# Seven half-size products for eight in a dense layer of 2048 tokens, on one core

## The chip, the cores and the metric

One core of a Trainium2 chip runs the whole kernel in one launch. The metric is the device time of one execution in microseconds (us), lower is better. All arithmetic keeps float32 accuracy: each matrix product is done as three products of halves of the operands (see below).

## The reference, cut to what matters

Two blocks, each added to its input. The first is a layernorm, a convolution of width 3 from 1024 to 768 channels, attention in blocks of 128 tokens with 16 heads of 64, and two projections. The second, which the change is about, is a layernorm and a dense layer with a gated low-rank term:

```python
y = jnp.einsum('bth,oh->bto', x, W_base) + b_base          # x: 2048 tokens x 1024, W_base 1024 x 1024
A = lora_A[active]; Bm = lora_B[active]                    # 4 active experts of 16, rank 8
z = jnp.einsum('bth,erh->bter', x, A)
contribs = jnp.einsum('bter,eor->bteo', z, Bm) * 2.0
logits = (jnp.einsum('bth,eh->bte', x, router_W) + router_b)[..., active]
alpha = jax.nn.softmax(jnp.log(domain_prior[active] + 1e-12) + logits, axis=-1)
return y + jnp.einsum('bteo,bte->bto', contribs, alpha)
# and outside: x1 = x + attention(layernorm(x));  out = x1 + this(layernorm(x1))
```

## The kernel before

Five instruction streams are written out by hand, one for each engine and one (SP) that issues DMAs; semaphores join them, and nothing reorders them. In order of time they do:

1. Layernorm, transposition and convolution (to some 260 us).
2. The attention, with eight groups of 256 tokens, each with eight pairs of heads. The function `attention_pair(D)` exists on TensorE (PE), VectorE (DVE), ScalarE (ACT) and GpSimd (POOL); each calls it for D = 1, 2, ..., and a call takes some 9.5 us. On DVE it does, in this order, `masked` (L1024), `heads_low` (`oT_lo`, L1036), `unit_out` (L1063, L1069), `reciprocals` (L1032), and at D = 5 and 6 `pw_lo` (L1114). PE waits for `oT_lo` before `output_sums` (L1457 to L1459). SP runs `attention_step(g, i)` (L432), two steps to one D, which issues loads and stores at fixed steps: `c_raw` of the next group at i = 7, the weights `W_base` (8 DMAs, L448) at (4, 0), and the gate's weights (L450 to L459) at (5, 0). The last are four groups of four DMAs, and each group reads the expert's number from `act_sb` into a register first.
3. The dense layer, in 16 tiles of 128 tokens. The normalised tile is turned on DVE (L1172) from `x1g` into `fxT`, and then split in two halves for PE: `xT_hi` by ACT (L775) and `xT_lo` by DVE (L1147). The weights are split in the same way into `fw_hi` (ACT) and `fw_lo` (DVE, L1206). They have 1060 columns: 36 for the gate (32 of the low-rank A, 4 of the router) and 1024 of `W_base`. `dense(t, b)` multiplies tile t by block b of the columns (354, 354 and 352 wide) with `three_pass`:

```python
pe.matmul(out, a_hi, b_hi, ...)   # L63
pe.matmul(out, a_lo, b_hi, ...)   # L64 (the order of the factors depends on the caller)
pe.matmul(out, a_hi, b_lo, ...)   # L65
```

That is 8 chunks x 3 blocks x 3 = 72 matmuls a tile. The gate's columns are in block 0. When it is done, DVE and ACT compute the softmax and the scaled z (L1180 to L1195) into `azs`; PE turns it (L1571), ACT copies it to `azsT`, and three matmuls with `b_stack` (L1578) add the low-rank term and the bias. DVE adds x1 (`tile_outputs`, L1202) into `y`, and POOL stores it (L586). `group_moments` (L1558) is a small matmul that spreads a tile's mean and scale over the layout of `x1g`; its input goes DVE `tile_statistics`, POOL `tile_power` (L533), DVE. `tile_transposes` turns tiles 0 and 1 on PE. SP loads a tile twice, as rows (`load_tile`, L419) and in groups (`load_groups`, L429).

Of the kernel before, what the change touches and what calls it, by code (L numbers as in the profile page):

```python
# [6 lines left out]
F32 = mybir.dt.float32  # L7
# [6 lines left out]
P = 128  # L14
# [10 lines left out]
EPS = 1e-5  # L25
# [62 lines left out]
def network(nc, ident, x, conv_w, conv_b, wq, wk, wv, wo, pw, bq, bk, bv, bo, pb, w_base, b_base, lora_a, lora_b, router_w, router_b,  # L88
            prior, active, c_dram, m_dram, x1, out):
# [66 lines left out]
    WZ = Z + DM  # L156
    NB = 3
    COLS = ((0, 354), (354, 708), (708, WZ))
    OFF = (Z, 0, 0)
    OUT = tuple((lo + off - Z, hi - Z) for (lo, hi), off in zip(COLS, OFF))  # L160
# [5 lines left out]

    def row(c):

        return (c - SOON) % DC

    with ExitStack() as ctx:
# [61 lines left out]
                                                               ("fxn_0", [P, DM], F32)))  # L233
        c_hi = (c0_hi, c1_hi)
# [3 lines left out]
        x1t_2, x1t_3 = place(nc, SH, (("x1t_2", [P, DM], F32), ("x1t_3", [P, DM], F32)))  # L238
        fw_hi, = place(nc, CY + 2 * size_of([P, MC, GT]) - size_of([P, DC, WZ]), (("fw_hi", [P, DC, WZ], F32R),))
        x1t = (x1t_0, x1t_1, x1t_2, x1t_3)  # L240
        fxn_1, rep, gmask, spread, gs = place(nc, XL, (("fxn_1", [P, DM], F32), ("rep", [P, P], F32), ("gmask", [P, TG], F32),
                                                       ("spread", [P, 2, TG, 2], F32), ("gs", [P, 2, TG, 2], F32)))
        x1g_0, x1g_1 = place(nc, XH + 4 * CHUNK, (("x1g_0", [P, TG, DM // TG], F32), ("x1g_1", [P, TG, DM // TG], F32)))
        x1g = (x1g_0, x1g_1)
        fxT, = place(nc, XH + 5 * CHUNK, (("fxT", [P, DM], F32),))
        fxn = (fxn_0, fxn_1)
        xT_hi, xT_lo = place(nc, XH + 2 * CHUNK, (("xT_hi", [P, 2, DC, P], F32R), ("xT_lo", [P, 2, DC, P], F32R)))
        y, = place(nc, XL + 2 * CHUNK, (("y", [P, 2, DM], F32),))
        b_raw, b_hi, b_lo, b_stack = place(nc, XH, (("b_raw", [ER + 1, DM], F32), ("b_hi", [ER + 1, DM], F32R), ("b_lo", [ER + 1, DM], F32R),
                                                    ("b_stack", [KB, DM], F32R)))  # L250

# [11 lines left out]
        tp = ((psum[:, 0], psum[:, 6]),) + ((psum[:, 0], psum[:, 3]),)  # L263
        yp = (tuple(psum[:, b] for b in (1, 2, 4)), tuple(psum[:, b] for b in (5, 6, 3)))
# [16 lines left out]
                 "active_loaded", "az_loaded", "b_loaded", "fw_loaded", "az_split_hi", "az_split_lo", "b_split_hi", "b_split_lo",  # L281
                 "b_stacked", "fw_hi_ready", "fw_lo_ready", "logp_in", "logp_ready", "lsum_ready",
                 "fstats_done", "fmv_done", "fvar_ready", "frstd_ready", "fxn_ready", "fturned", "xT_hi_ready", "xT_lo_ready",
                 "spread_ready", "gp_done", "gs_ready", "z_done", "logit_ready", "fmax_ready", "fexp_ready", "rec_ready", "alpha_ready", "az_ready", "azs_hi_ready", "azs_ready",
                 "azT_done", "azsT_ready", "y_done", "y_ready")
        s = {n: sp.sem(n) for n in names}
        f_loaded = [sp.sem(f"f_loaded{i}") for i in range(XS)]
# [45 lines left out]
        def by_group(a, t):  # L333
            return a.rearrange("p c t -> p (c t)") if t < BLOCKED else a.rearrange("p c (g q) -> p c g q", g=TG)
# [1299 lines left out]
```

## Time and profile before

| | us |
|---|---|
| median of 3 runs (lowest, highest) | 786.25 (786.21, 786.28) |
| the profiled execution, its own time | 786.38 |
| its span in the trace | 784.5 |
| PE busy in the span | 765.6 (98%) |
| DVE busy | 524.7 (67%) |
| ACT busy | 382.3 (49%) |
| POOL busy | 165.5 (21%) |
| dense layer, from its first products to the end | about 575 to 784.5 |

The span is measured in the trace from the first to the last recorded work; the execution's own time lies 1.9 us around it. "Busy" counts overlapping matmuls as one stretch. A row of the timeline gives the start and the length of one or more instructions of a kind; matmuls overlap, so their cost is the distance from one start to the next, not the length.

### The profile page before, as it was taken

To read this page: it belongs to the slowest core of one execution; us is meant where nothing else is said; L and a number is where in the kernel's file an instruction comes from. 1 tells how busy PE (TensorE), PEld (TensorE's weight loads), DVE (VectorE), ACT (ScalarE), POOL (GpSimd) and SP (SyncE) were. 2 spreads that over 40 slices of the span, in tenths; PEclk is the share of its full clock that TensorE was granted. 3 is DMA by queue.
4 is the path that set the end of the run, shared out by engine and by line. 5 is a ranking of instruction groups with operands and counts; after the bars stand their busy time and mean duration, and the time that the engine had idled before them with its cause. 6 is when DMAs were issued, how large, how long until landed. Compare 5 with 4: busy or idle time off the path is not lost.

```text
span 784.5 us, 14391 instructions
## 1 busy us (share of the span) xinstructions
PE 765.6 (98%) x5182; PEld 693.8 (88%) x5182; DVE 524.7 (67%) x1506; ACT 382.3 (49%) x1046; POOL 165.5 (21%) x170
## 2 busy tenths in 40 slices
PE   4999999999999999999999999999999999999996
PEld 3898888888888889989999989899889999999996
DVE  6999996889887966454544445545787666767652
ACT  5953442344344887676767676767950111111010
POOL 2300100000000236252535344352401111111100
PEclk9999999999999999999999999999999999999999
DMA  8846834434446230403072332102254443525301
GB/s 329 287 123 176 271 116 133 170 127 161 156 153 242 88 122 1 148 2 140 10 265 99 99 112 96 55 33 78 95 152 146 147 136 107 158 85 162 108 28 54
DMA packets 49435, 101.39 MB, mean 129 GB/s; under 512 B 10195, under 2 KB 26451, under 8 KB 48084
## 3 DMA queue, kind: packets, MB, share of 16 engines
q1 hardware_dynamic: 47060, 92.08, 35.5%
q0 software_dynamic: 2304, 8.39, 2.6%
q8 instruction: 42, 0.69, 0.4%
q14 instruction: 29, 0.24, 0.1%
HBM read 73.97 MB, written 26.08 MB: 128 GB/s over the span
## 4 chain that ended last, share of the span: by engine, by line
PE 93%; DVE 3%; ACT 2%; issue 1%; DMA 0%; POOL 0%; DVEq 0%; POOLq 0%
PE net_psum L63 21%; PE net_psum L65 21%; PE net_psum L64 21%; PE net_psum L1342 11%; PE net_psum L1404 4%; PE net_psum L1415 4%; PE net_psum L1427 4%; PE net_psum L1457 2%; PE net_psum L1458 2%; PE net_psum L1459 2%; PE net_psum L1326 1%; PE net_psum L1578 1%; ACT pr L683 1%; ACT xn L609 1%; DMA xn<-in_x 0%
## 5 line engine op out<-in xcount | busy, mean ns | idle before, releaser
L63 PE MATMUL net_psum<-fw_hi,xT_hi 128*128 128x354 f32 (+1 forms) x384 | 127.2, 331 | 0.4 <-DVE fw_lo L1206 0.4
L64 PE MATMUL net_psum<-fw_lo,xT_hi 128*128 128x354 f32 (+1 forms) x384 | 124.2, 324 | 0.0
L65 PE MATMUL net_psum<-fw_hi,xT_lo 128*128 128x354 f32 (+1 forms) x384 | 124.2, 323 | 0.0
L547 POOL TENSOR_TENSOR pr<-pr,rrec 128x512 f32<-128x512 f32 x64 | 66.6, 1042 | 209.2 <-DVE rrec L1032 206.1
L683 ACT ACTIVATE pr<-pr,negmax 128x128 f32<-128x128 f32 x256 | 99.0, 395 | 1.0 <-DVE negmax L1024 1.0
L1342 PE MATMUL net_psum<-ua,wa 128*128 128x256 f32 x384 | 83.8, 379 | 0.5 <-DVE ua L914 0.5
L1024 DVE CUSTOM_DVE_ANT_0 pr<-net_psum,mask 128x128 f32<-128x128 f32 x256 | 57.2, 288 | 37.9 <-PE net_psum L1404 37.8
L1342 PEld LDWEIGHTS net_psum<-ua,wa 128*128 128x128 f32 x384 | 72.6, 190 | 10.3 <-issue 0.7
L63 PE MATMUL net_psum<-x_hi,w_hi 128*128 128x512 f32 x192 | 76.4, 398 | 0.0
L64 PE MATMUL net_psum<-x_lo,w_hi 128*128 128x512 f32 x192 | 76.2, 397 | 0.0
L65 PE MATMUL net_psum<-x_hi,w_lo 128*128 128x512 f32 x192 | 75.6, 394 | 0.0
L63 PE MATMUL net_psum<-c_hi,wqk_hi 128*128 128x256 f32 x256 | 74.2, 290 | 0.0
L63 PEld LDWEIGHTS net_psum<-fw_hi,xT_hi 128*128 128x128 f32 x384 | 72.2, 188 | 1.5 <-DVE fw_lo L1206 0.8
L64 PEld LDWEIGHTS net_psum<-fw_lo,xT_hi 128*128 128x128 f32 x384 | 72.4, 189 | 0.0
L65 PEld LDWEIGHTS net_psum<-fw_hi,xT_lo 128*128 128x128 f32 x384 | 72.3, 188 | 0.0
L64 PE MATMUL net_psum<-c_lo,wqk_hi 128*128 128x256 f32 x256 | 71.6, 280 | 0.0
L65 PE MATMUL net_psum<-c_hi,wqk_lo 128*128 128x256 f32 x256 | 71.6, 280 | 0.0
L775 ACT ACTIVATE xT_hi<-fxT 128x512 fp32r<-128x512 f32 x28 | 16.1, 625 | 110.8 <-DVE fxT L1172 110.8
L640 ACT ACTIVATE w_hi<-raw 128x1024 fp32r<-128x1024 f32 x24 | 25.5, 1062 | 85.1 <-PE net_psum L65 76.7
L702 ACT ACTIVATE oT_hi<-net_psum,net_bv_c 128x256 fp32r<-128x256 f32 x64 | 26.9, 472 | 56.9 <-PE net_psum L1415 56.9
L1202 DVE TENSOR_TENSOR y<-net_psum,x1t 128x318 f32<-128x318 f32 (+2 forms) x48 | 21.7, 508 | 47.8 <-PE net_psum L1578 47.8
L683 ACT ACTIVATION_READ_ACCUMULATOR pr<-pr,negmax 128x1 f32 x256 | 49.7, 194 | 0.0
(194 smaller groups left out, 1772.3 us busy)
## 6 DMA issues: line engine op xcount, KB each, us to landing
wa<-in_conv_w SPq DMA_DIRECT2D x24, 512.0 KB, 4.1
raw<-in_conv_w SPq DMA_DIRECT2D x24, 384.0 KB, 4.2
xn<-in_x SPq DMA_DIRECT2D x16, 512.0 KB, 10.2
xr<-in_x SPq DMA_DIRECT2D x8, 1024.0 KB, 5.0
x_scratch<-xr SPq DMA_DIRECT2D x8, 1024.0 KB, 4.1
x1t<-x_scratch SPq DMA_DIRECT2D x16, 512.0 KB, 4.1
out<-y POOLq DMA_DIRECT2D x16, 512.0 KB, 5.0
x1g<-x_scratch SPq DMA_DIRECT2D x56, 128.0 KB, 3.2
```

The source lines that it names most:

```text
L63: pe.matmul(out, w_hi, x_hi, start=first, stop=False)
L64: pe.matmul(out, w_hi, x_lo, start=False, stop=False)
L65: return pe.matmul(out, w_lo, x_hi, start=False, stop=last)
L547: pool.tensor_tensor(pr[:, jj % 4], pr[:, jj % 4], rrec[:, jj % 4].unsqueeze(2).to_broadcast([P, UN, P]), ALU.mult).then_inc(s["p_ready"], 1)
L640: act.activation(w_hi[:, k % WR], raw[:, k % RR, 1:5], ACT.Copy).then_inc(s["w_hi_ready"], 1)
L683: e = act.activation(pr[:, jj % 4, un], pr[:, jj % 4, un], ACT.Exp, bias=negmax[:, jj % 2, un:un + 1], scale=-1.0, accum_out=rsum[:, jj % ...
L702: act.activation(oT_hi[:, jj % 2], op[:, jj % 2].rearrange("p b t -> p (b t)"), ACT.Identity, bias=bv_c[:, jj % NP:jj % NP + 1]).then_inc( ...
L1024: m = dve.tensor_tensor_reduce(out=pr[:, jj % 4, un], in0=scp[:, h, jj % 2 * GT + b * P:jj % 2 * GT + (b + 1) * P], in1=mask[:], scale=-DH ...
L1342: mm = pe.matmul(duo_acc(d, mi)[:, v * QUADS:(v + 1) * QUADS], wa[:, a % AW, mi, 1 - v, c % 2], ua[:, c, v, n * QUADS:(n + 1) * QUADS], st ...
L1404: mm = pe.matmul(scp[:, h, o], qf[e, jj % 2, t], kf[e, jj % 2, t], start=True, stop=True)
L1415: mm = pe.matmul(op[h * DH:(h + 1) * DH, jj % 2, b], vf[:, b, j * P + h * DH:j * P + (h + 1) * DH], pT[:, jj % 2, b, h * P:(h + 1) * P], s ...
L1427: mm = pe.transpose(ptp[jj % 2][:, un * P:(un + 1) * P], pr[:, jj % 4, un], ident[:])
```

## The change

The first CL = 4 tiles run as before, with blocks of 284, 512 and 264 columns. The other 12 run as NQ = 6 pairs. A pair's product is seen as a 2 x 2 matrix of blocks (two tiles by two halves of the 1024 channels) times a 2 x 2 matrix (two halves of the channels by two halves of the columns, 532 each: 18 + 512 and two of padding), and done with seven products of blocks instead of eight (the Strassen-Winograd scheme). The products are named A11, S1, S2, A12, S3, A22, S4 by their left operand; the S ones are sums and differences of turned tiles, made on DVE (`operand_sum`), and their right factors for S1, S2, S3, and for S4, are differences of blocks of the weights. The results are added in pieces by `pair_sum` on DVE, in place in the x1 tile, and stored from there.

The sums of the weights are made during the attention, one chunk each in `attention_pair(6)` to `(21)` (`weight_sum` and `low_sum` on DVE, `high_sum` on ACT), stored to DRAM by SP, and loaded again after the attention. For that the weights `W_base` and the gate's weights are loaded at SP's step (1, 0), and `gate_weights` on DVE copies the gate's columns into place in `attention_pair(5)`. The statistics of paired tiles move from DVE to ACT (`tile_moments`) and POOL (`pair_moments`), the scaling from DVE to ACT (`pair_scale`).

The diff, cut to its core:

```diff
@@ SP: attention_step
-                if (g, i) == (4, 0):
-                    for c in range(DC):
-                        sync.dma_start(fw_raw[:, row(c), Z:WZ], w_base[:, c]).then_inc(s["fw_loaded"], 16)
-                if (g, i) == (5, 0):
-                    sync.dma_start(act_sb[:], active).then_inc(s["active_loaded"], 16)
+                k = (NP * g + i) // 2 - TFIRST - 1
+                if i % 2 and 0 <= k < TSUMS:
+                    store_sum(k)
+                if (g, i) == (5, 7):
+                    for k in range(2):
+                        sync.wait_ge(t_stored[k], 16 * TSUMS)
                     load_tile(0)
                     load_tile(1)
+                if (g, i) == (1, 0):
+                    sync.dma_start(act_sb[:], active).then_inc(s["active_loaded"], 16)
+                    for c in range(DC):
+                        for (lo, hi), off, (left, right) in zip(COLS, OFF, OUT):
+                            sync.dma_start(fw_raw[:, row(c), lo + off:lo + off + right - left], w_base[:, c, left:right]).then_inc(s["fw_loaded"], 16)
                     sync.wait_ge(s["active_loaded"], 16)
                     for e in range(E_ACT):
@@ SP: after the attention
-            for t in range(XS, TT):
+            load_sums(0)
...
+            load_sums(1)
+            load_sums(2)
+            load_pair(0)
+            load_pair(1)
+            load_sums(3)
+            for q in range(2, NQ):
+                load_pair(q)
+            for n, (t, j) in enumerate(((TT - 2, 0), (TT - 2, 1), (TT - 1, 0), (TT - 1, 1))):
+                lo, hi = ((0, 2 * YW), (2 * YW, DM))[j]
+                sync.wait_ge(s["y_ready"], summed(NQ - 1, n + 5))
+                sync.dma_start(out[t * P:(t + 1) * P, lo:hi], x1t[x_slot(t)][:, lo:hi]).then_inc(s["last_stored"], 16)
@@ POOL
-            for t in range(TT):
-                if t + 2 < TT:
+            for t in range(CL):
+                if t + 2 < CL:
                     tile_power(t + 2)
                 store(t)
+                if t == CL - 2:
+                    pair_moments(0)
@@ DVE: attention_pair
+                if D == TFIRST - 1:
+                    gate_weights()
+                if 0 <= D - TFIRST < TSUMS:
+                    weight_sum(D - TFIRST)
+                if 0 <= D - TFIRST - 1 < TSUMS:
+                    low_sum(D - TFIRST - 1)
                 if D in (5, 6):
                     dve.wait_ge(s["pw_hi_ready"], D - 4)
+            def gate_weights():
+                dve.wait_ge(s["az_loaded"], 64 * E_ACT)
+                dve.memset(fw_raw[:, :, 3 * QW - PAD:3 * QW + PAD], 0.0)
+                half, pair = ER // 2, E_ACT // 2
+                for h in range(2):
+                    dve.tensor_copy(fw_raw[:, :, QW * h:QW * h + half], a_raw[:, :, half * h:half * h + half])
+                    z = dve.tensor_copy(fw_raw[:, :, QW * h + half:QW * h + ZW], r_raw[:, pair * h:pair * h + pair].rearrange("p e c -> p c e"))
@@ DVE: the pairs
+            for q in range(NQ):
+                more = q + 1 < NQ
+                a = CL + 2 * q
+                if q:
+                    pair_sum(q - 1, 5)
+                    pair_sum(q - 1, 6)
+                low_operand(q, S2)
+                pair_sum(q, 1)
+                low_operand(q, A12)
+                operand_sum(q, S4)
+                pair_sum(q, 2)
+                low_operand(q, S3)
+                if q:
+                    pair_sum(q - 1, 7)
+                    pair_sum(q - 1, 8)
+                low_operand(q, A22)
+                pair_sum(q, 3)
+                low_operand(q, S4)
+                if more:
+                    pair_turn(q + 1, 0)
+                pair_sum(q, 4)
+                if more:
+                    pair_turn(q + 1, 1)
+                    operand_sum(q + 1, S1)
+                gate_scores(a)
+                if more:
+                    low_operand(q + 1, A11)
+                    operand_sum(q + 1, S3)
+                gate_inputs(a)
...
@@ PE
+            def product(q, o, bank, chunks=range(DC // 2)):
...
+                for c in chunks:
+                    for h in range(2):
...
+                        pe.matmul(to, x_hi, b_hi, start=c == 0 and o in (A11, S1, A12), stop=False, skip_group_check=True)
+                        pe.matmul(to, x_hi, b_lo, start=False, stop=False, skip_group_check=True)
+                        mm = pe.matmul(to, x_lo, b_hi, start=False, stop=c == DC // 2 - 1, skip_group_check=True)
...
+            for q in range(NQ):
+                a = CL + 2 * q
+                product(q, A11, XB)
+                if q:
+                    gate_turn(a - 1)
...
+                product(q, S1, ZB)
+                if q:
+                    low_rank(q - 1, 1)
+                product(q, S2, XB)
+                if q + 1 < NQ:
+                    pair_moments(q + 1)
+                product(q, A12, YB, range(0, 2))
+                product(q, S3, XB)
+                product(q, A12, YB, range(2, 4))
+                product(q, A22, XB)
+                product(q, S4, ZB, range(0, 2))
+                gate_turn(a)
+                product(q, S4, ZB, range(2, 4))
+                low_rank(q, 0)
+            gate_turn(TT - 1)
+            low_rank(NQ - 1, 1)
```

On SP's queue, behind the load of group 2's `c_raw`, before:

```order
L370 DMA c_raw<-c_scratch 128x6x256 [waits net_c_lo_ready,net_c_stored]
L438 DMA pb_r<-in_pb 128x1024
L440 DMA xr<-in_x 128x2x1024
L370 DMA c_raw<-c_scratch 128x6x256 [waits net_c_lo_ready]
L435 DMA x_scratch<-xr 128x2x1024 [waits net_x1_ready]
```

and after (eight triples of `fw_raw` stand there, and four groups from L608 to L612, of which the last has no other behind it but L585):

```order
L472 DMA c_raw<-c_scratch 128x6x256 [waits net_c_lo_ready,net_c_stored]
L602 DMA act_sb<-in_active 1x4
L605 DMA fw_raw<-in_w_base 128x248
L605 DMA fw_raw<-in_w_base 128x512
L605 DMA fw_raw<-in_w_base 128x264
...
L608 TENSOR_LOAD act_sb [waits net_active_loaded]
L609 DMA a_raw<-in_lora_a 128x8x8
L610 DMA r_raw<-in_router_w 128x8
L611 DMA lbias<-in_router_b 128x1
L612 DMA lbias<-in_prior 128x1
...
```

The loads for the gate have moved from behind the fifth group to here, ahead of `pb_r` and the first `xr`.

On DVE, in `attention_pair(5)`, before:

```order
L1032 RECIPROCAL rrec<-rsum 128x4 [waits net_p_ready,net_exp_ready] x2
L1063 COPY vf<-net_psum 128x512 [waits net_v_done]
L1114 TENSOR_TENSOR pw_lo<-pw_raw,pw_hi 128x1024 [waits net_pw_hi_ready]
L1024 ISA pr,negmax<-net_psum,mask 128x128 [waits net_pT_done,net_sc_done]
L1024 ISA negmax 128x1
```

and after:

```order
L1310 RECIPROCAL rrec<-rsum 128x4 [waits net_p_ready,net_exp_ready] x2
L1341 COPY vf<-net_psum 128x512 [waits net_v_done]
L1403 MEMSET fw_raw 128x8x4 [waits net_az_loaded]
L1406 COPY fw_raw<-a_raw 128x8x16
L1407 COPY fw_raw<-r_raw 128x8x2
L1406 COPY fw_raw<-a_raw 128x8x16
L1407 COPY fw_raw<-r_raw 128x8x2
L1398 TENSOR_TENSOR pw_lo<-pw_raw,pw_hi 128x1024 [waits net_pw_hi_ready]
L1302 ISA pr,negmax<-net_psum,mask 128x128 [waits net_pT_done,net_sc_done]
```

Five instructions and a wait for all sixteen gate loads now stand ahead of `pw_lo` and of the next masks.

On PE, the end of the program before (the last of the matmuls with 352 columns, and the low-rank term):

```order
L63 MATMUL net_psum<-fw_hi,xT_hi 128x352
L64 MATMUL net_psum<-fw_lo,xT_hi 128x352
L65 MATMUL net_psum<-fw_hi,xT_lo 128x352
L1578 MATMUL net_psum<-b_stack,azsT 128x318 [waits net_azsT_ready]
L1578 MATMUL net_psum<-b_stack,azsT 128x354
L1578 MATMUL net_psum<-b_stack,azsT 128x352
```

and after (266 columns a matmul; L2016 is the transposition of the last tile's `azs`):

```order
L2003 MATMUL net_psum<-fw_hi,xT_lo 128x266
L2027 MATMUL net_psum<-b_stack,azsT 128x248 [waits net_azsT_ready]
L2027 MATMUL net_psum<-b_stack,azsT 128x248
L2027 MATMUL net_psum<-b_stack,azsT 128x264 x2
L2016 MATMUL net_psum<-ident,azs 98x128 [waits net_y_ready,net_azs_ready]
L2027 MATMUL net_psum<-b_stack,azsT 128x248 [waits net_azsT_ready]
L2027 MATMUL net_psum<-b_stack,azsT 128x248
L2027 MATMUL net_psum<-b_stack,azsT 128x264 x2
```

The last tile's transposition stands behind the last product, with nothing left to run beside it.

## Rows read from the trace of the kernel before

**Rows 1.** The chain that ended last, share of the span by engine (the page).

```profile
PE 93%; DVE 3%; ACT 2%; issue 1%; DMA 0%; POOL 0%; DVEq 0%; POOLq 0%
```

**Rows 2.** Window of one tile: length; busy (count) by engine; PEclk, DMA, GB/s.

```profile
653.90:666.34 12.44, 12.44 (x80) 12.40 (x79) 8.19 (x25) 1.71 (x5) 1.60 (x2) 1.00 0.45 126
```

**Rows 3.** Timeline of PE, tile 6: start, length, line, op, names, shapes, count.

```profile
654.54 0.32 PE L65 MATMUL net_psum<-fw_hi,xT_lo 128*128 128x354 f32 x1
...
661.85 0.33 PE L65 MATMUL net_psum<-fw_hi,xT_lo 128*128 128x354 f32 x1
```

**Rows 4.** Timeline of PE, matmuls of 256 columns in the attention.

```profile
347.53 0.28 PE L64 MATMUL net_psum<-c_lo,wqk_hi 128*128 128x256 f32 x1
...
348.71 0.28 PE L65 MATMUL net_psum<-c_hi,wqk_lo 128*128 128x256 f32 x1
```

**Rows 5.** Groups of DVE, 614 to 733 us: count | busy, mean ns | idle before.

```profile
L1172 DVE STREAM_TRANSPOSE fxT<-x1g 128x1024 f32<-128x1024 f32 x10 | 12.4, 1245 | 0.9
L1147 DVE TENSOR_TENSOR xT_lo<-fxT,xT_hi 128x512 fp32r<-128x512 f32 x18 | 11.5, 683 | 0.0
```

**Rows 6.** Timeline of DVE, the gate of tile 8, from its scores to `azs`.

```profile
683.21 0.16 DVE L1180 TENSOR_TENSOR logit<-net_psum,lsum 128x4 f32<-128x4 f32 x1 [0.25 <-PE net_psum L65]
...
684.45 0.16 DVE L1184 RECIPROCAL erec<-esum 128x1 f32<-128x1 f32 x1 [0.89 <-ACT expl L779]
...
685.36 0.19 DVE L1195 TENSOR_TENSOR azs<-az,azs 128x32 fp32r<-128x32 f32 x1
```

**Rows 7.** Timeline of PE, the end of dense(0, 0).

```profile
575.03 0.43 PE L63 MATMUL net_psum<-fw_hi,xT_hi 128*128 128x354 f32 x1 [0.38 <-DVE fw_lo L1206]
```

**Rows 8.** Timeline of POOL: one tile's moments, and the store of tile 2.

```profile
27.83 0.19 POOL L511 TENSOR_SCALAR cvareps<-csq 128x1 f32<-128x1 f32 x1 [0.44 <-ACT junk L602]
...
29.05 0.19 POOL L515 TENSOR_TENSOR cshift<-csum,crstd 128x1 f32<-128x1 f32 x1
...
618.18 0.67 POOL L586 DMA_DIRECT2D out<-y  x1 [4.67 <-DVE y L1202]
```

**Rows 9.** DMA issues of the page: kind, count, KB, us from issue to landing.

```profile
x1t<-x_scratch SPq DMA_DIRECT2D x16, 512.0 KB, 4.1
```

**Rows 10.** Group of ACT, 0 to 60 us.

```profile
L602 ACT ACTIVATE junk<-xn,csum 128x1024 f32<-128x1024 f32 x4 | 4.6, 1151 | 0.1
```

**Rows 11.** Timeline of POOL, the last store.

```profile
779.80 0.53 POOL L586 DMA_DIRECT2D out<-y  x1 [11.69 <-DVE y L1202]
```

**Rows 12.** Timeline of SP: start, length of the issues, line, names, count.

```profile
275.23 0.37 SPq L370 DMA_DIRECT2D c_raw<-c_scratch  x1
...
397.26 4.23 SPq L448 DMA_DIRECT2D fw_raw<-in_w_base  x8
...
443.17 0.69 SPq L456 DMA_DIRECT2D a_raw<-in_lora_a  x1
...
455.05 0.38 SPq L459 DMA_DIRECT2D lbias<-in_prior  x1
```

**Rows 13.** DMA issues, as in rows 9, of the last of the gate's loads.

```profile
lbias<-in_prior SPq DMA_DIRECT2D x4, 0.5 KB, 2.5
```

**Rows 14.** Timeline of DVE in `attention_pair(5)` and `(6)`.

```profile
293.07 1.71 DVE L1114 TENSOR_TENSOR pw_lo<-pw_raw,pw_hi 128x1024 fp32r<-128x1024 f32 x1
...
296.54 0.88 DVE L1036 SCALAR_TENSOR_TENSOR oT_lo<-net_psum,net_bv_c,oT_hi 128x256 fp32r<-128x256 f32 x2
```

**Rows 15.** Timeline of PE, the first matmul that reads that `oT_lo`'s tile.

```profile
302.10 0.28 PE L1457 MATMUL net_psum<-oT_hi,wo_hi 128*128 128x256 f32 x1
```

**Rows 16.** Windows of 1 us behind the last matmul, columns as in rows 2.

```profile
781.00:782.00 1.00, 0.00 (x0) 0.00 (x0) 0.00 (x0) 0.00 (x0) 0.00 (x0) 0.99 0.98 406
782.00:783.00 1.00, 0.00 (x0) 0.00 (x0) 0.00 (x0) 0.00 (x0) 0.00 (x0) 0.50 0.17 70
```

**Rows 17.** Timeline of SP at the start of the kernel.

```profile
9.13 7.21 SPq L345 DMA_DIRECT2D xn<-in_x  x8
```

More of the change, by code:

```diff
@@ L250, in network @@
                                                     ("b_stack", [KB, DM], F32R)))
+        t_rows = []
+        for name, at, count in (("t_v", XL + 3 * CHUNK, 13), ("t_p", XL, 5), ("t_b", XH, 5), ("t_f", XL + 6 * CHUNK + 3 * size_of([P, DM]), 1)):
+            t_rows += place(nc, at, [(f"{name}{i}", [P, 2 * QW], F32R) for i in range(count)])
         psum = sp.ps("psum", [P, 8, BANK])
@@ L850, in _ @@
+            for t in range(CL):
+                if t and t + 1 < CL:
                     tile_xT(t + 1)
@@ L1558, in group_moments, with pair_moments @@
                 pe.matmul(gp, rep[:], spread[:, t % 2], start=True, stop=True).then_inc(s["gp_done"], 1)
-            for t in range(TT):
+            def pair_moments(q):
+                pe.wait_ge(s["spread_ready"], CL - BLOCKED + 2 * (q + 1))
+                pe.wait_ge(s["gs_ready"], CL - BLOCKED + q)
+                if q:
+                    pe.wait_ge(s["y_ready"], summed(q - 2, 7) if q > 1 else NB * CL)
+                pe.matmul(gpq[q % 2], rep[:], spread[:].rearrange("p k g v -> p (k g v)"), start=True, stop=True).then_inc(s["gp_done"], 1)
@@ new lines, in low_rank @@
+            def low_rank(q, k):
+                t = CL + 2 * q + k
+                pe.wait_ge(s["azsT_ready"], t + 1)
+                for j in range(2):
+                    new = k == 1 and j == 1
+                    bank = xyz[1 - q % 2][XB] if new and q == NQ - 1 else xyz[q % 2][((YB, ZB), (XB, YB))[k][j]]
+                    for h in range(2):
+                        cols = slice(YW * h, YW * h + YW) if j == 0 else slice(2 * YW + RW * h, 2 * YW + RW * h + RW)
+                        mm = pe.matmul(bank_half(bank, j)[:, h], azsT[:, t % 2], b_stack[:, cols], start=new, stop=True, skip_group_check=True)
+                    mm.then_inc(s["y_done"], 1)
@@ L1561, in _ @@
+            for t in range(CL):
                 if t:
-                    if t + 1 < TT:
+                    if t + 1 < CL:
                         group_moments(t + 1)
                     dense(t, 0)
+                    if t == CL - 1:
+                        pair_moments(0)
                     dense(t, 1)
```

464 lines of the change are left out of this document (397 added, 67 removed).

## The prediction, made before the changed kernel had run

> **What bounds the kernel now.** I read the chain of waits first: 93% of the span goes through PE [rows 1]. Then the window of one dense tile: PE is busy for all of its 12.44 us, DVE for 8.2, ACT for 1.7 and POOL for 1.6 [rows 2]. So the dense layer is worth what its matmuls take, and there is room on the other engines. Next the distances between matmuls. With 354 columns 45 intervals take 661.85 - 654.54 = 7.31 us, 0.162 us each [rows 3]; with 256 columns 10 intervals take 1.18 us, 0.118 each [rows 4]. Every one of these has its own weight load, so the price goes by columns: 0.00045 us a column, and 0.1225 us for 266 columns.
>
> **Six pairs of tiles.** Before, a pair costs 2 x 12.44 = 24.89 us. Of one tile's 12.44, the 72 products take 11.7, three low-rank matmuls 3 x 0.16 = 0.5, and what is left for a transposition and a moments matmul is 0.27. Now a pair has 7 x 4 x 2 x 3 = 168 products of 266 columns instead of 144 of 353: 168 x 0.1225 = 20.58. With 8 low-rank matmuls of some 256 columns (8 x 0.119 = 0.95), two transpositions and one moments matmul (0.4 by the 0.27 above), the PE work is 21.9 us.
>
> Does DVE keep up? It gets 7 `low_operand`, 4 `operand_sum` and 8 `pair_sum` of about 512 columns, 19 x 0.64 = 12.2 us at 11.5/18 each [rows 5], two turns of 1.25 [rows 5], and the small gate operations, 1.7 for each tile (0.5 for the scores, 1.1 from the reciprocal to `azs`, plus 0.1 for an operation more [rows 6]): 18 of 22 us. That fits on average, so only the order can hurt. I laid the four streams out with these durations. The tightest place is the gate's transposition in the middle of product S4. PE comes to it 19.9 us into the pair (156 products, four low-rank matmuls, the moments and one transposition: 156 x 0.1225 + 0.5 + 0.2 + 0.1). The input that starts DVE's last stretch is product S3, which ends at 14.0; behind it stand `pair_sum(4)`, a turn, a sum, the scores, `low_operand`, a sum and the gate's inputs: 4 x 0.64 + 1.25 + 0.5 + 1.2 = 5.5 us. Started at 14.2, it would be 0.2 us early; but DVE comes to it 0.4 us late by the operations ahead, so PE waits 0.2 to 0.3 us a pair. I take 22.2 us a pair: 6 x (24.89 - 22.2) = **-16.1 us**. ACT has 14 of 22 us, and its sums hide behind PE. Bounds: with no wait -18; with DVE's operations a tenth longer the hand order gives 0.35 us of wait a pair, with a fifth 0.85, and a stop of 1.5 a pair gives -8.
>
> By the Trainium skill ("TensorE: Matmul & The Clock Gate", the list of what overlaps and what doesn't in the part on packing) a weight load overlaps matmuls "only when row_grp differs". All the loads here use every row, so by that rule each of the 24 additional loads of a pair would stand in PE's way. The rows speak against it: 256-column matmuls, each with a load of its own, start every 118 ns [rows 4], which leaves no time for an unhidden load. By the rule the result would be rival E below.
>
> **The way into the pairs: +4.0 us.** dense(0, 0) already waits 0.38 us for the last `fw_lo` [rows 7]. It is now 284 columns wide, some 0.75 us shorter, but ends by the same `fw_lo`: +0.7. In tile 3 PE comes to `pair_moments(0)` at about 620.0. On POOL its two tiles stand behind the store of tile 2, issued 618.18 to 618.85 [rows 8], and take 1.4 us each for three operations (27.83 to 29.24 [rows 8]) and 0.3 for the `spread`: 618.9 + 3.4 = 622.3, which PE waits for, +2.1. The second, `pair_moments(1)`, needs tile 7, whose load is issued when tile 3's outputs are done (about 633.1 by then), lands 4.1 us later [rows 9], goes through two passes of 1.15 us on ACT [rows 10] and 1.8 on POOL: 641.3, against 640.1 for PE, +1.2. The sums of the weights for S4 land about 640.8 and are wanted at 646: nothing. New widths in the single tiles move the number of columns by none and the number of matmuls by none: nothing, +-0.5. Bounds of the whole: +0.7 to +6.
>
> **The end: +0.7 us.** The last transposition, the copy to `azsT` and the low-rank matmuls of the last tile have no product beside them (0.75 us); against this the tile is stored in halves by SP rather than whole by POOL, whose issue took 0.53 [rows 11]. Bounds 0 to +1.5.
>
> **The attention: +6.7 us.** SP issues the load of `c_raw` at 275.23 and is free at 275.6 [rows 12]. Now `act_sb` and 24 DMAs of `W_base` come next. They take 0.37 (the `c_raw` row) to 0.53 us (4.23/8 for the same tensor [rows 12]); I take 0.45 between them: 276.1 + 24 x 0.45 = 286.9. Then come the four groups with register reads. From the first `a_raw` to the end of the last issue they took 455.43 - 443.17 = 12.3 us [rows 12], to which come about 0.9 us of reads ahead of the first and 2.5 us to the last landing [rows 13], in all 15.3 to 15.7. So all sixteen have landed at 302.2 to 302.9. DVE comes to `gate_weights`, which waits for them, at 293.07, where `pw_lo` stood before [rows 14]. It waits 9 to 10 us. Behind that instruction stand the gate's copies (0.75 us, an estimate from their 256 and 32 columns at the rate of rows 5), then the row of before again: `pw_lo` and eight masks, 296.54 - 293.07 = 3.5, less 0.2 as the masks no longer wait, and `oT_lo`, 0.87 [rows 14]. PE wants this for `output_sums` at 302.10 [rows 15] and gets it at 302.3 + 0.75 + 3.3 + 0.87 = 307.2: **+5.1**. With 0.37 and 0.53 an issue it is 2.7 and 7. The first `weight_sum` (532 columns) and the second `pw_lo` then stand ahead of `a_lo`, which a projection needs: +0.8 (0 to 1.5). From D = 6 to 22 DVE has 1.2 us more a call, which fits into idle stretches, and ACT 0.55: nothing.
>
> In such a stop PE's clock may fall. At the end of the run the granted clock is 0.99 in the window that ends 782 and 0.50 in the next [rows 16], the lower of its two levels (1.2 of 2.4 GHz), after PE had done nothing since its last matmul at 778.4. A stop of 5 us may end with the clock low; then the matmuls behind it take up to twice their time until it rises again. What that costs is not in these rows: estimate +0.8, bounds 0 and 3.
>
> **Sum.** -16.1 + 4.0 + 0.7 + 5.1 + 0.8 + 0.8 = -4.7. From the profiled execution's 786.38 that gives 781.7, and the median lies 0.13 under it: **781.5 us**.
>
> **The rivals.**
>
> B. The gate's loads are not waited for to any effect: SP issues faster, or PE's own reserve takes it up. For it speaks the 9 us between DVE's `pw_lo` and PE's `output_sums` [rows 14, 15]; against it that the wait is as long. Then the attention costs nothing: 786.25 - 16.1 + 4.0 + 0.7 = 774.8 us.
>
> C. The other side: SP issues at the rate at which it issued `xn`, 7.21/8 = 0.9 us a DMA [rows 17], since all 24 loads of `W_base` are queued at once, 4.3 MB. Each 0.1 us an issue moves the landing and so PE by 2.4 us. At 0.9 PE is 10.8 us later than in the forecast: 792.3. From 0.65 us an issue on the change is slower than the kernel before. Against it: eight of these loads, four times the size of the small ones, took 0.53 each [rows 12].
>
> D. The pairs are limited by DVE, not PE. If the operations on the stretch before the transposition take more than in rows 5 (two sources of PSUM, strided pieces), each pair stops for 1.5 us more: 781.5 + 9 = 790.5. For it: the chain has 0.2 us to spare only. Against it: rows 5 hold operations with strided sources already.
>
> E. The weight loads count: a matmul cannot start sooner than 0.14 us after the last one, between the 0.118 of rows 4 and the 0.162 of rows 3, however few its columns. Then a pair costs 168 x 0.14 + 1.35 = 24.9 us, as before, and the result is 781.5 + 16 = 797.5. Against it: the interval of rows 4 itself.
>
> By the skill's page of above a load of 128 columns takes 107 ns (P / 1.2 GHz); 24 more of them a pair would be 2.6 us, and the result 797, an estimate from that page's figure.
>
> **How the numbers follow.** Forecast (A) 0.52, with its own range 777 to 786; B 0.27; C 0.10; D 0.08; E 0.03. A measurement of this kernel tells 0.2% (1.6 us) from no change. By its bounds A is faster in 0.46, no change in 0.05 and slower in 0.01; B is faster; C and D have 0.02 and 0.01 of no change, where their price is half as large, and are slower in the rest; E is slower. Sums: faster 0.73, same 0.08, slower 0.19. The range takes A and B with their bounds and leaves out most of C and E: 771.5 to 789.
>
> **What would show it right or wrong.** In the profile of the changed kernel: the distance of two matmuls of 266 columns (0.1225 us), the length of a pair from one product A11 to the next (22.2 us) and what idle time stands before the gate's transposition (0.2 to 0.3 us); idle time of PE before the two moments matmuls (2.1 and 1.2 us); idle time of DVE before its memset in `attention_pair(5)` (9 to 10 us, ended by a load of the gate's weights) and of PE before `output_sums` of `attention_pair(6)` (5 us); SP's issues of `fw_raw` (0.45 us each). The forecast fails upwards if these issues take 0.6 us or more, or if the pair takes over 23; it fails downwards if PE does not wait there at all.

## The result, and the profile after

The changed kernel is slower: 792.52 us median (790.63 to 793.49, 4 runs) against 786.26, ratio 1.0076 (95% interval 1.0062 to 1.0091). The forecast was 781.5 with a range up to 789. The profiled execution took 790.63 us, its span is 788.9. So the traces explain 4.4 us of the 6.3; the rest is that the profiled execution was the fastest of four that scatter over 3 us, where the kernel before scatters over 0.2. Times of a stage are read below in the one profiled execution of each kernel.

The pairs themselves came out as computed. The window of one pair, from one tile's low-rank term to the same of the next pair (columns as in [rows 2]):

```profile
693.30:715.51 22.21, 22.21 (x183) 22.21 (x182) 17.06 (x43) 13.69 (x31) 4.42 (x10) 1.00 0.44 146
```

22.21 us for two tiles, where [rows 2] have 12.44 for one. PE is busy throughout, DVE for 17.1, ACT for 13.7. The products, answering to [rows 3, 4] (timeline of PE; 23 intervals between the first row and the last, 0.124 us each):

```profile
671.53 0.29 PE L2001 MATMUL net_psum<-fw_hi,xT_hi 128*128 128x266 f32 x1
...
674.39 0.29 PE L2003 MATMUL net_psum<-fw_hi,xT_lo 128*128 128x266 f32 x1
```

All in order, then, from the first pair on. Now what PE waits for before that (the view of waits over the whole run: us in all, times, longest; left out are three rows that both kernels have, 12.5 us in all, and 0.4 us at the end, for which see below):

```profile
PE net_psum L1990 <- POOL spread L768: 7.3, 2, 6.6
PE net_psum L1882 <- DVE oT_lo L1314: 5.5, 1, 5.5
PE net_psum L63 <- DVE a_lo L1321: 1.1, 3, 0.4
PE net_psum L63 <- DVE fw_lo L1587: 1.1, 2, 0.6
```

Before, of these rows only `fw_lo` stood there, with 0.4 us. The first row is the way into the pairs, the second the forecast stop in `attention_pair(6)`.

**The attention, 10.4 us later.** (A call of `attention_pair` takes 10.1 to 10.4 us by the distances of the scores, not the 9.5 of the description above.) The timelines of SP, DVE and PE, which answer to [rows 12, 14, 15]:

```profile
276.00 12.26 SPq L605 DMA_DIRECT2D fw_raw<-in_w_base  x24
...
301.04 0.38 SPq L612 DMA_DIRECT2D lbias<-in_prior  x1
```

```profile
303.87 0.09 DVE L1403 MEMSET fw_raw<- 128x32 f32 x1 [10.85 <-DMA lbias<-in_prior]
...
311.37 2.84 DVE L1398 TENSOR_TENSOR pw_lo<-pw_raw,pw_hi 128x1024 fp32r<-128x1024 f32 x1
```

```profile
307.62 0.58 PE L1882 MATMUL net_psum<-oT_hi,wo_hi 128*128 128x256 f32 x1 [5.49 <-DVE oT_lo L1314]
```

SP takes 12.26/24 = 0.51 us an issue, the last load has landed at 303.87 and PE stops for 5.49 us: forecast 0.45, 302.3 and 5.1. What the forecast put at 1.6 more was 3.2: the scores of the next-but-one call start 8.7 us later than before (322.40 for 313.72), 3.2 us more than the stop. The windows behind the stop show the clock in it:

```profile
307.00:308.00 1.00, 0.38 (x2) 0.38 (x2) 1.00 (x5) 1.00 (x7) 0.00 (x0) 0.50 0.52 213
308.00:313.00 5.00, 5.00 (x34) 4.55 (x35) 4.06 (x6) 3.79 (x14) 4.21 (x3) 0.50 0.01 4
313.00:314.00 1.00, 1.00 (x14) 0.96 (x10) 1.00 (x1) 0.22 (x1) 1.00 (x2) 0.59 0.00 0
```

The granted clock is 0.50, the 1.2 of 2.4 GHz, when PE starts again, and stays so for some 6 us. Then, three times with four calls between them, a projection is late by 0.37 us (PE, DVE and POOL around the first):

```profile
358.05 0.47 PE L63 MATMUL net_psum<-pw_hi,a_hi 128*128 128x512 f32 x1 [0.37 <-DVE a_lo L1321]
```

```profile
352.36 1.02 DVE L1421 TENSOR_TENSOR t_raw<-fw_raw 128x532 f32<-128x532 f32 x1
353.30 2.33 DVE L1425 TENSOR_TENSOR t_low<-t_raw,t_hi 128x532 fp32r<-128x532 f32 x1
```

```profile
352.76 2.30 POOL L696 TENSOR_TENSOR c_lo<-c_raw,c_hi 128x768 fp32r<-128x768 f32 x1
```

The distance between the scores of the calls around it grows by 0.58 us, so 1.75 in all. `t_low` takes 0.70 us elsewhere and 2.33 here, and ends at 355.63, 0.57 us after POOL's `c_lo` (355.06). By the Trainium skill ("SBUF — State Buffer", "SBUF: two separate sides") a VectorE operation with two SBUF inputs and a GpSimd operation that reads SBUF exclude each other for a whole instruction. The trace agrees: 2.33 us is the rest of `c_lo`, 1.76 us, and then most of `t_low`'s own 0.70. The forecast had 1.2 us of DVE work a call and did not ask what POOL does beside it.

**The way in, 8.5 us.** Tile 3's low-rank term starts 19.8 us later than before (648.46 for 628.62), tile 2's 11.4 (627.54 for 616.18). The timeline of SP, then of ACT, POOL and PE:

```profile
600.11 8.63 SPq L560 DMA_DIRECT2D t_v<-t_scratch  x13
608.79 2.49 SPq L560 DMA_DIRECT2D t_p<-t_scratch  x5
611.32 2.65 SPq L560 DMA_DIRECT2D t_b<-t_scratch  x5
614.01 0.55 SPq L560 DMA_DIRECT2D t_f<-t_scratch  x1
614.61 6.88 SPq L531 DMA_DIRECT2D x1g<-x_scratch  x8
621.59 0.87 SPq L521 DMA_DIRECT2D x1t<-x_scratch  x2
```

```profile
631.45 1.06 ACT L1057 ACTIVATE fjunk<-x1t 128x1024 f32<-128x1024 f32 x1 [6.35 <-DMA x1t<-x_scratch]
```

```profile
636.47 0.19 POOL L761 TENSOR_SCALAR pvar<-pcsq 128x1 f32<-128x1 f32 x1 [1.12 <-ACT fjunk L1059]
```

```profile
637.90 0.61 PE L1990 MATMUL net_psum<-spread,rep 128*128 128x16 f32 x2 [6.57 <-POOL spread L768]
...
658.73 0.40 PE L1990 MATMUL net_psum<-spread,rep 128*128 128x16 f32 x2 [0.71 <-POOL spread L768]
```

The rows of tiles 4 and 5 are issued last, behind 24 loads of weight sums and 8 of groups, and the first is there for ACT 9.8 us after its issue, not 4.1 [rows 9]. ACT's passes start at 631.45, POOL waits for ACT (1.12 us), and PE's moments start at 637.90. The clock is at 0.50 again from 635 to 641. The second moments wait 0.71 us.

**The end.** The last matmul is over at about 783.9 and the span ends 5.0 us later, where it was 6.1. The last tile now goes out in two halves, and from SP rather than POOL; which of the two wins the time was not separated. The shifts add up to the difference of the spans: +10.4 (attention), +0.9 (to tile 0's low-rank term), +8.5 (way in), -15.4 (from there to the end) = +4.4.

### The profile page after: what moved, and what is told of

Same layout as the page of the kernel before. It is cut to its first block and busy times, and to the rows that moved or that the text cites. A ratio compares the mean times of both kernels' runs of the same rounds, so it can differ in the third digit from the quotient of the medians.

```text
span 788.9 us, 15051 instructions
## 1 busy us (share of the span) xinstructions
PE 756.0 (96%) x5326; PEld 677.9 (86%) x5326; DVE 563.8 (71%) x1503; ACT 454.4 (58%) x1180; POOL 176.3 (22%) x204
## 5 line engine op out<-in xcount | busy, mean ns | idle before, releaser
L1767 PEld LDWEIGHTS net_psum<-ua,wa 128*128 128x128 f32 x384 | 72.6, 190 | 10.4 <-issue 0.8
L64 PEld LDWEIGHTS net_psum<-c_lo,wqk_hi 128*128 128x128 f32 x256 | 48.2, 188 | 1.3
L63 PEld LDWEIGHTS net_psum<-c_hi,wqk_hi 128*128 128x128 f32 x256 | 48.1, 188 | 1.2
L1310 DVE RECIPROCAL rrec<-rsum 128x4 f32<-128x4 f32 x64 | 11.3, 177 | 52.3 <-ACT pr L883 52.1
L65 PEld LDWEIGHTS net_psum<-c_hi,wqk_lo 128*128 128x128 f32 x256 | 48.2, 188 | 0.0
L65 PEld LDWEIGHTS net_psum<-x_hi,w_lo 128*128 128x128 f32 x192 | 36.3, 189 | 8.7
L64 PEld LDWEIGHTS net_psum<-x_lo,w_hi 128*128 128x128 f32 x192 | 36.2, 188 | 8.5
L63 PEld LDWEIGHTS net_psum<-x_hi,w_hi 128*128 128x128 f32 x192 | 35.9, 187 | 8.8
L1576 DVE TENSOR_TENSOR x1t<-net_psum,x1t 128x528 f32<-128x528 f32 (+1 forms) x48 | 32.1, 689 | 15.7 <-PE net_psum L2003 15.7
## 6 DMA issues: line engine op xcount, KB each, us to landing
xn<-in_x SPq DMA_DIRECT2D x16, 512.0 KB, 10.1
```

The source lines that it names most:

```text
L63: pe.matmul(out, w_hi, x_hi, start=first, stop=False)
L64: pe.matmul(out, w_hi, x_lo, start=False, stop=False)
L65: return pe.matmul(out, w_lo, x_hi, start=False, stop=last)
L1576: dve.tensor_tensor(half_of(tile, j), bank_half(b, j), half_of(tile, j), ALU.add).then_inc(s["y_ready"], 1)
L1767: mm = pe.matmul(duo_acc(d, mi)[:, v * QUADS:(v + 1) * QUADS], wa[:, a % AW, mi, 1 - v, c % 2], ua[:, c, v, n * QUADS:(n + 1) * QUADS], st ...
```

## The experiments

Each was timed with the kernel before on the same chip.

**1. Sums a call later.** `TFIRST = 7` for 6: `gate_weights` then stands in `attention_pair(6)`.

```diff
-    TFIRST, TSUMS = 6, 16
+    TFIRST, TSUMS = 7, 16
```

> The first weight sum, and with it the wait for the gate's sixteen loads, moves from attention_pair(5)/(6) to (6)/(7); nothing else is changed. Theory: PE's stop of 5.5 us before the output sums of attention_pair(6), and the 6.8 us at half clock behind it (3.2 us lost), both come from DVE waiting there for loads that land at 303.9. A call later DVE arrives at about 303, so it waits about 1 us, PE's clock stays at 1.00, and the profiled execution gets 8 to 8.7 us shorter than 790.6: about 782.5. Rival: the loads or pw_lo hold up the first projection instead, PE stops about as long two calls later, and the time stays within 2 us of 790.6.

785.84 us median (784.37 to 789.07), ratio 0.9998 (0.9989 to 1.0007); profiled 784.37, 6.3 us less and not 8. PE's stop is gone and its clock stays at 1.00 from 302 to 312. But the loads delay the first `a_lo` by 0.8 us, and there is a fourth late projection. One constant gives back all that the change had lost against the kernel before: the two medians, 785.84 and 786.36, cannot be told apart.

**2. Rows of tiles 4 and 5 first.** On SP, `load_tile(4)` ahead of `load_sums(1)` and `(2)`, `load_tile(5)` behind them.

> SP loads the rows of tiles 4 and 5 as soon as their buffers are free, tile 4 ahead of the second and third eight loads of weight sums, tile 5 behind them, instead of both last. Theory: PE's 6.6 us before the first moments of a pair, and the low clock behind it (1.6 us), come from the row load of tile 4, issued at 621.6 behind 24 loads of sums and 8 group loads and landed only at 631.4. With the row loads early the wait falls to about 2 us (what ACT's two passes and POOL's chain take behind tile 2), the clock stays at 1.00, and the execution is 5.5 to 6.5 us shorter: 784 to 785. Rival: ACT's passes and POOL's chain set it whenever the rows land: the wait stays above 5 us and the time within 1 us of 790.6.

789.07 us (ratio 1.0046, 1.0032 to 1.006). The wait fell from 6.57 to 4.47 us only. Tile 4's row was there in time; tile 5's, issued at 619.9 behind 16 loads of sums, took 11.4 us and ended ACT's wait at 631.3, as before. The row's landing is what is waited for, then, and the edit was half of what it needed.

**3. Sums earlier in the call.** `weight_sum` and `low_sum` right behind `heads_low`.

> Within each call on DVE, weight_sum and low_sum stand right behind heads_low instead of at the end of the call. Theory: PE's three late projections (0.37 us of wait each, 0.58 with the refill, 1.8 us in all) come from a low_sum that takes 2.33 instead of 0.70 us while POOL's c_lo runs (352.8 to 355.1) and so delays a_lo. Moved to a place where POOL is idle, every low_sum takes 0.7 us, the three waits go, and the execution is 1.8 us shorter: about 788.8. Rival: it is DVE's amount of work in those calls, not the overlap: the waits stay or move, time within 0.5 us of 790.6.

794.10 us (1.0093, 1.0078 to 1.0109). The 16 `low_sum` take 0.705 us in the mean, and PE's three waits for `a_lo` are gone. The edit also takes `low_sum` away from its place ahead of `a_lo`, so the run alone does not tell the place from the length; but the 1.6 us that `low_sum` had been longer beside POOL are more than the 0.37 us that PE waited. And a new wait came, on DVE and PE:

```profile
375.38 0.71 DVE L1421 TENSOR_TENSOR t_raw<-fw_raw,t_raw 128x532 f32<-128x532 f32 x1 [4.93 <-DMA t_scratch<-t_low]
```

```profile
336.05 0.66 PE L1852 MATMUL net_psum<-ident,pr 128*128 128x128 f32 x4 [1.60 <-POOL pr L715]
```

DVE comes so early to `weight_sum` that its buffer's store is not done, 22 us in four waits, and `rrec`, POOL's `pr` and PE's turns stand behind it.

**4. The stop kept busy.** The value product ahead of the stop done four times.

```diff
-                for c in range(WC):
+                for c in list(range(WC)) * times:
...
-                    values(e, n) if is_v else projection(e, n)
+                    values(e, n, 4 if (D, k) == (6, 1) else 1) if is_v else projection(e, n)
```

> The value product that stands just ahead of PE's stop in attention_pair(6) is done four times over (18 more matmuls of 512 columns, 4.2 us of PE work in the 5.5 us of the stop). Theory: the 3.2 us that PE loses between 307.6 and 313.8 are the clock alone, which fell because PE was idle; kept busy, the clock stays at 1.00, the stop's end stays at 307.6, and the execution is 3 us shorter: about 787.5. Rival: the 3.2 us are DVE's and ACT's lateness behind the stop: the time stays at 790.6 or goes up.

792.93 us (1.0083, 1.0069 to 1.0097), profiled 792.00: nothing gained. The clock did stay at 1.00, and the scores behind the stop start 1.6 us earlier (308.84 for 310.48), of which 0.34 are because the stop itself ended so much earlier (307.28; the loads had landed sooner). But the next ones start at 322.01 for 322.40, only those 0.34 us earlier, since PE now waits for `a_lo`, 2.1 us at once (windows, waits and DVE's timeline):

```profile
308.00:310.00 2.00, 1.57 (x18) 1.26 (x17) 1.06 (x5) 1.92 (x9) 1.54 (x2) 1.00 0.00 0
```

```profile
PE net_psum L63 <- DVE a_lo L1321: 3.3, 4, 2.1
```

```profile
311.03 2.85 DVE L1398 TENSOR_TENSOR pw_lo<-pw_raw,pw_hi 128x1024 fp32r<-128x1024 f32 x1
```

So my theory that these 3.2 us were the clock alone falls: DVE's backlog behind its own stop, with `pw_lo` at 2.85 us beside POOL, is as long. DVE starts `a_lo` at 314.64 for 314.97, again 0.33 us earlier, whatever PE's clock; the slow matmuls only hid the wait for it.

**5. low_sum in the next call.** On top of 1, the `low_sum` ahead of each `a_lo` at the end of the next call.

```diff
+                if q == 3 and 0 <= D - TFIRST - 2 < TSUMS:
+                    low_sum(D - TFIRST - 2)
                 if 0 <= D - TFIRST < TSUMS:
                     weight_sum(D - TFIRST)
-                if 0 <= D - TFIRST - 1 < TSUMS:
+                if q != 2 and 0 <= D - TFIRST - 1 < TSUMS:
```

> On top of the kernel whose sums start a call later (784.4 profiled, 785.8 median): the low_sum that stands ahead of each a_lo goes to the end of the next call; the order of the operations is the same, only the place of that one among the attention's moves. Theory: the four waits of 0.39 us for a_lo (0.58 each with what follows) come from this low_sum running against POOL's c_lo, 2.33 us instead of 0.70. Without it ahead of a_lo they go, and nothing else waits: 2.3 us less, profiled 782.1. Rival (as moving all the sums ahead in the call showed, 792 to 794): DVE has no free place in these calls, and a wait for POOL's pr or for oT_lo takes their place: 784.4 or more.

785.82 us (0.9994, 0.9985 to 1.0003), the same as 1. The four late `a_lo` are gone, and three waits for ACT's `kf` (1.4 us) have come: the rival in kind, though it had named `pr` or `oT_lo`. PE also waits 1.1 us for POOL's `c_lo` at 319 here. That is not this edit's: it stands in 6, 7 and 8 too (0.95 to 1.11 us), not in 1, and experiment 9 turns to it.

**6. Rows before the last sums.** On top of 1; and POOL's `pair_moments(0)` ahead of the store of tile 2.

```diff
-            load_sums(2)
-            load_pair(0)
+            for t in (CL, CL + 1):
+                sync.wait_ge(s["y_ready"], NB * (t - CL + 1))
+                load_tile(t)
+                load_groups(t)
+                load_sums(t - CL + 1)
             load_pair(1)
```

> On top of the kernel whose sums start a call later: the rows and groups of tile 4 are loaded ahead of the second eight weight sums and those of tile 5 ahead of the third eight; on POOL the moments of the first pair stand ahead of the store of tile 2. Theory: the load of a row lands when what was issued before it has been moved (tile 5 landed 11.4 us after its issue behind 16 loads of sums), so both rows now land before ACT is free at about 617.6 on this kernel's clock, and PE's wait before the first moments goes from 6.7 to under 1 us; the second wait of 0.75 stays at 0.7 to 1.5. With the refill at a low clock 6.5 to 8 us less: profiled 777 to 778. Rival: ACT's two passes a tile and POOL's chain take until 4 us after PE comes there: 781 to 782.

777.96 us (0.989, 0.9875 to 0.9905), 7.9 less than experiment 1. PE's wait before the first moments is gone altogether. The profiled execution, 779.55, has a longer second wait instead:

```profile
625.42 0.40 PE L1991 MATMUL net_psum<-spread,rep 128*128 128x16 f32 x2
...
646.15 0.61 PE L1991 MATMUL net_psum<-spread,rep 128*128 128x16 f32 x2 [2.25 <-POOL spread L769]
```

Two things were changed at once, the rows and POOL's order. Experiment 8 shows what the second is worth.

**7. All of 1, 5 and 6.**

> All edits together: sums a call later, low_sum in the next call, rows before the last sums, POOL's moments before the store. If the causes are independent the savings add: 784.4 - 2.3 - 7 = about 775 profiled, 1.4% under the kernel before, and its executions vary by less than the 3 us of the changed kernel, since nothing then waits on a DMA. Rival: one of the gaps reappears at the next place (the second pair's moments, the last fw_lo): 779 or more.

778.63 us (0.9909, 0.9894 to 0.9924), profiled 776.85, scatter 4.4 us: no better than 6, and my expectation that the scatter goes was wrong.

**8. Eight single tiles.** `CL = 8` on top of 1.

> CL = 8 in the kernel whose sums start a call later: eight single tiles and four pairs instead of four and six. Theory: a pair costs PE 22.2 us and two single tiles 24.9, so two pairs fewer cost 5.4 us; and the rows of the first pair no longer queue behind 24 loads of sums, so most of the 6.7 us wait and its low clock (8.3 us in all) goes: 784.4 + 5.4 - 7 = about 783 profiled. Rival: the wait ahead of the first pair belongs to ACT and POOL and stays: 789.8.

785.30 us (0.9985, 0.9976 to 0.9994), profiled 784.55; 783 was expected. The wait ahead of the first pair is 1.7 us, so the other 5 were the queue on SP. The timelines of POOL and PE show what is left (`out<-y` is the store of tile 6):

```profile
673.37 0.53 POOL L754 DMA_DIRECT2D out<-y  x1 [11.80 <-DVE y L1583]
673.97 0.19 POOL L761 TENSOR_SCALAR pvar<-pcsq 128x1 f32<-128x1 f32 x1
...
676.61 0.20 POOL L768 TENSOR_TENSOR spread<-prs,gmask 128x8 f32<-128x8 f32 x1
```

```profile
676.86 0.40 PE L1990 MATMUL net_psum<-spread,rep 128*128 128x16 f32 x2 [1.68 <-POOL spread L768]
```

With the rows in time POOL goes from its store straight into the two tiles' moments, and PE waits 1.68 us for them. This is the chain of the forecast, which had 2.1 for it. In experiment 6 POOL's edit takes it away, so of the 7.9 us won there some 1.7 are that edit's (an estimate from the row above, since it was not timed alone). The second moments wait 1.73 us here, and a pair costs 22.2 us as before.

**9. Gate loads behind xr.** `TFIRST = 8`, the weight loads at SP's step (1, 3), with the edits of 6.

```diff
-                if (g, i) == (1, 0):
+                if (g, i) == (1, 3):
                     sync.dma_start(act_sb[:], active).then_inc(s["active_loaded"], 16)
```

> The weight loads on SP stand behind pb_r and the first xr (step (1, 3) instead of (1, 0)), and the sums start one call later still (8; their end and load_tile(0) move to step (6, 1)); with rows before the last sums and POOL's moments before the store, low_sum in its own call. Theory: the 1.1 us that PE waits for POOL's c_lo at 319 comes from xr, issued at 302 instead of 276 and landed 3 to 5 us after POOL wants it; and the 0.8 us for a_lo at 309 from the gate's copies and pw_lo in the call ahead of it. Both go; what stays are the four late projections: 777 profiled less 2 to 2.5 and plus nothing, about 776, and the executions lie closer together than 3 us because no engine waits for a DMA in the attention. Rival: the executions' scatter and these waits come from elsewhere (row loads in the dense layer): the time stays at 777 to 778 and the scatter at 3 us.

778.19 us (0.9888, 0.987 to 0.9907), profiled 778.73. In the attention it did what it should: PE's waits for POOL's `c_lo` and for the first `a_lo` are gone, and tile 0's low-rank term starts at 594.36 for 596.59 in 6. The median is no better than that of 6, though: in the profiled execution the gain was spent on the second pair's moments, which wait 3.61 us.

**10. The same with the edit of 5.**

> The same with low_sum in the next call ahead of each a_lo. Theory: as in the run of that edit alone its gain of 4 x 0.58 us is given back by ACT's kf (1.5 us in three waits), since high_sum on ACT waits for a later weight_sum: within 1 us of the kernel without it. Rival: the three waits come from the late xr and go with it: 2.3 us shorter, about 774.

777.27 us (0.9879, 0.9859 to 0.99): within 1 us of 9, with 2.3 us of waits for `kf` in place of 1.6 for `a_lo`.

**11. No fourth sums.**

> The kernel of the run before last (e9) without the last eight loads of weight sums and without PE's wait for them: the right factor of the product S4 is then not the difference of blocks but the plain weights, a part of the computation that is left out. Theory: the second pair's moments wait for tile 7's row, which took 5.8 and 7.0 us to land because these eight loads are issued right behind it and share the DMA engines; in other executions it lands faster, and this is where the scatter of 3 us comes from. Without them the row lands in about 4 us, PE's wait goes from 3.6 to under 1 us, profiled 775 to 776, and the executions lie within 1 us. Rival: the row lands as late and the scatter stays; then it is not this contention.

775.85 us (0.9872, 0.9855 to 0.9888), profiled 774.42, for a kernel that leaves a part of the computation out. The wait fell from 3.6 to 0.9 us, but the scatter is still 2.3 us, so the eight loads are not its only cause. Tile 7's row landed in 4.4 us here, but in 4.2 in 7 as well, where the eight loads stand behind it.

**12. Row of tile 6 first.** On 9, complete.

```diff
-            load_pair(1)
+            sync.wait_ge(s["y_ready"], NB * 3)
+            load_tile(6)
+            load_groups(6)
+            load_groups(7)
+            sync.wait_ge(s["y_ready"], NB * 4)
+            load_tile(7)
```

> The same kernel, complete, with the row of tile 6 loaded as soon as its buffer is free, ahead of the groups of tiles 6 and 7. Theory: only tile 7's row, which cannot be issued before tile 3's outputs, ends the wait before the second pair's moments, so this changes nothing but ACT's first two passes: 776 to 779 as e9, same scatter. Rival: ACT's four passes in a row are what PE waits for, and with the first two done early it comes 2 us sooner: 775 to 776.5.

774.34 us (774.08 to 775.09), ratio 0.9851 (0.9835 to 0.9867): the best version, 1.5% under the kernel before, and the four executions lie within 1.0 us. The time is the rival's, or a little better. The timelines of ACT in 9, and of ACT, SP and PE in this one:

```profile
641.24 1.06 ACT L1058 ACTIVATE fjunk<-x1t 128x1024 f32<-128x1024 f32 x1 [2.44 <-DMA x1t<-x_scratch]
```

```profile
638.39 1.06 ACT L1063 ACTIVATE fjunk<-x1t 128x1024 f32<-128x1024 f32 x1 [1.54 <-DMA x1t<-x_scratch]
```

```profile
620.99 0.32 SPq L521 DMA_DIRECT2D x1t<-x_scratch  x1
...
634.20 0.34 SPq L521 DMA_DIRECT2D x1t<-x_scratch  x1
```

```profile
642.33 0.40 PE L1996 MATMUL net_psum<-spread,rep 128*128 128x16 f32 x2 [0.66 <-POOL spread L774]
```

The rival's reason, four passes of ACT in a row, is not what the rows show: in 9 as well ACT had done its first two passes and stood idle for 2.44 us when tile 7's row came. That row was issued at 634.2 in both. It took 7.0 us to ACT in 9 and 4.2 here, 2.8 us less, which is nearly all of the 2.95 us by which PE's wait is shorter; the two early passes gave next to nothing in this execution. Nor is the quick landing shown to be the edit's: in 7, 10 and 9, which load tiles 6 and 7 in one and the same order, tile 7's row took 4.2, 5.7 and 7.0 us, and PE's wait was 0.66, 2.35 and 3.61 us. What speaks for the edit is that none of its four executions is long.

## Why the prediction was wrong, point by point

- **The six pairs, -16.1: right.** 22.21 us a pair for 22.2. In part by luck: a product takes 0.124 us and not 0.1225 (+0.3 a pair), and the wait of 0.2 to 0.3 us before the gate's transposition does not exist, so two errors cancel. Rival D, DVE as the bound, is out. So is E, by which the weight loads count: 183 matmuls with a full load each fit into 22.21 us. The rule of the Trainium skill weighed there ("TensorE: Matmul & The Clock Gate", the part on packing) does not hold for these loads: matmuls with a load each start every 0.124 us.
- **The attention, +6.7: mis-sized, 10.4.** SP's issue times were near (0.51 for 0.45, not rival C's 0.9). The stop's length (5.49 for 5.1) owes something to luck: the last load landed 1.6 us later than computed, and from there to `output_sums` it took 3.75 us, not 4.9. Behind the stop 3.2 us for 1.6: the half clock, and under it DVE's backlog of the same length (experiment 4). And 1.75 us for "nothing" from the later calls, whose `low_sum` met POOL's `c_lo` (experiment 3). One more mechanism was left out of the sum: the gate's loads stand ahead of `pb_r` and `xr` on SP, and where the stop is gone POOL, and so PE, comes late by 1 us at 319 (experiments 5 to 8, not 9). It cost nothing in the changed kernel itself.
- **The way in, +4.0: the step that failed.** "In tile 3 PE comes to `pair_moments(0)` ... On POOL its two tiles stand behind the store of tile 2": that was given as all there is to wait for, +2.1 (its own figures, 620.0 and 622.3, make it 2.3). The chain on POOL is real, 1.68 us in experiment 8, but another ends last: the rows of tiles 4 and 5, which the forecast did not follow at all, though it followed tile 7's with a landing of 4.1 us. They stand behind 24 loads of 266 KB on the same queue and reach ACT 9.8 us after the issue, 11.4 in experiment 2. The step was worth 6.57 us and the refill at half clock, 8.5 in all. Experiments 2, 6 and 8 show it: with tile 4's row alone moved the wait is 4.5, with no 24 loads ahead of the rows it is 1.7, and with both rows and POOL's moments moved it is nothing, and 7.9 us are won. The 0.7 us of tile 0 came as computed in its waits (0.46 and 0.61 for 0.38); its low-rank term is 0.9 us later, of which 0.2 stay open.
- **The second moments, +1.2: right in kind, too large.** 0.71 us in the changed kernel, 0.66 to 3.61 where the first wait is gone, by the landing of tile 7's row. A term that hangs on a DMA's landing is a range, not a value. Some of the executions' scatter sits here; how much was not measured, as only one execution of each kernel has a trace.
- **The end, +0.7: wrong in sign.** PE's part came (0.37 us of wait and the matmuls), but from the last matmul to the end 1.1 us are won.
- **The range.** Up to 789 it allowed one cause to fail. Both stops of PE came with their low clock, and the sum over two such terms went beyond it: the profiled execution is 8.9 us over its forecast of 781.7, by 6.4 for the first moments, 3.7 for the attention, and 1.2 back behind them. What the median has over the profiled execution, 1.9 us, stays open; in no trace here is it seen. The clock of the unprofiled executions is a hint only: in experiment 7 the mean granted clock was 1.000 in the shortest (776.85 us) and 0.993 in the longest (781.23), as if the long one had one more stop with a low clock.

## What to carry to other kernels

A change that moves loads must be followed as a queue: for every load behind the moved ones, when it is issued, what is in flight ahead of it, and who waits for it; a landing time of the trace of before was good only for a queue as empty as it was there. The saved matmuls were worth just what the intervals said, and more than that was lost, nearly all of it in two stops of PE at places where the program changes its stage; moving one constant, a few loads and POOL's moments was the cure. Where several chains end at one wait, compute each of them: here the right chain was worked out and a longer one beside it was not seen. And where PE stops while its feeder is late as well, as here, a low clock behind the stop has no price of its own: with PE kept busy the next wait took the same time.

## What had not been expected of the hardware

- A DVE operation from SBUF to SBUF that starts beside one of POOL's ends only after it, by about its own length or less: `t_low` took 2.33 us for 0.70 and ended 0.6 after POOL's, `pw_lo` 2.84 for 1.22 and 1.1 after. A copy with one input did the same in experiment 1: 128 columns in 1.37 us for 0.21, ended 0.1 after POOL's.
- A row of 512 KB, 4.1 us from issue to landing on a quiet queue, took 9.8 behind 24 loads of 266 KB and 8 of 128 KB, and 11.4 behind 16 of 266 KB that had just been issued. With one and the same order of the queue it took 4.2, 5.7 and 7.0 in three kernels.
- PE came back at half clock after idle stretches of 5.5 and 6.6 us, and also of 2.25 us (experiment 6: 0.54 in the window from 646 and 0.50 from 647). The clock stayed at 1.00 after 0.7 us, and also after 2.13 us in experiment 4 (windows from 314 to 320).
- The changed kernel's executions scatter by 3 us, those of experiment 12 by 1.0, those of the kernel before by 0.2.
